# Twelve source-row tiles of each graph layer fetched row by row by SyncE

## The chip, the cores and the metric

The kernel runs on one core of one Trainium2 chip. The metric is the device time of one launch in microseconds (us). The kernel before takes 4936.72 us, the median of 3 runs (4935.95 to 4943.19).

## The reference, cut to what matters

Node features x are 12500 x 256, and there are 200000 edges (src, dst, edge_weight), sorted by dst. The graph block has two layers of this form, followed by normalizations and a residual:

```python
def _hconv(x, src, dst, ew, w1, b1, w2, b2, g, b):
    h = jax.nn.relu(x @ w1 + b1)
    msg = ew[:, None] * h[src]                                  # one row of h for each edge
    agg = jax.ops.segment_sum(msg, dst, num_segments=x.shape[0])
    h = agg @ w2 + b2
    return jax.nn.relu(_bn(h, g, b))
```

Behind it comes a mixture of 8 experts, each with three products of 256 x 256 over all nodes, weighted by a softmax. All is in 32-bit floats; the large products of the experts and with w2 are made of three partial products of split operands.

## The kernel before, in words

The stages follow one another: `first_layer` (layer norm, the product with w1, h to DRAM, and the edge tables), `aggregate(0)`, `second_layer`, `aggregate(1)`, and then `experts`, which takes the rest. The change touches the tables and the two aggregations.

Edges are cut into tiles of 128 (P), and four tiles (GT) make a group of 512 edges: 1563 tiles, 391 groups. Destinations grow quadratically, so the first groups go to few nodes. Those are treated in another way: layer 0 treats 112 groups so, layer 1 128 (FGL). For them the kernel builds dense weight sheets ("front", in DRAM), and SyncE loads them in batches: `load(a)` (L985) loads four blocks of 128 rows of h (L998) and the matching part of a sheet (L1000) into one of two buffers. TensorE's `unit` (L1067) multiplies one block; the last unit of a batch frees the buffer (semaphore f_mm), for which the load after the next waits (L995). A pass over the nodes is 25 batches; layer 0 has 4 passes, layer 1 has 5.

The other groups (279 in layer 0, 263 in layer 1, numbered q) go through gathers. GpSimd's `gather(t)` (L1020) fetches the 128 rows of h that tile t needs with one indirect DMA (L1025), into one of 16 slots (R). Before it overwrites a slot it waits for the product of the group that used it (semaphore g_mm). VectorE builds one-hot matrices with the edge weights (L1263, L1269); TensorE multiplies rows and one-hots of a group (L1109) when all four tiles have landed; VectorE adds the sums to `agg` (L1389) at an offset that it loads into registers, sixteen at a time (L1372, L1373).

The order is written at build time. `place(level)` assigns each unit to a group q, so that TensorE's estimated work per group is level; `unit_at` holds the result. TensorE's program is then, for each q: the products of the group, the products that build sheets (L1063, in the early groups), the units assigned to q, and late in the layer the products with w2. SyncE's program in an aggregation is only `for n in range(NF): load(n)`.

The edge tables src_col, rel_col and ew_col have four parts of GW = 512 columns, one column for each group; 391 of the 512 are used.

Of the kernel before, what the change touches and what calls it, by code (L numbers as in the profile page):

```python
def build(nc, a, out):
# [8 lines left out]
    P = 128  # L10
# [8 lines left out]
    GT = 4  # L19
# [3 lines left out]
    GW = GB * P  # L23
    NB = -(-N // P)
# [68 lines left out]
    def sem(name):  # L93
        return top.enter_context(nc.semaphore(name))
# [58 lines left out]
    with top:  # L153
# [65 lines left out]
        def first_layer():  # L219
            with ExitStack() as s:  # L220
# [79 lines left out]
                with nc.Block() as block:  # L300
# [88 lines left out]
                    def _(g):  # L389
# [5 lines left out]
                        for i in range(NCH + 4):  # L395
# [40 lines left out]
                            if I_TURN <= i < I_TURN + NT:  # L436
                                what, bs = turns[i - I_TURN]
                                dstbuf = {"src": src_col, "ew": ew_col, "dst": rel_col, "front": None}[what]
                                g.wait_ge(side_p, TURNS + i - I_TURN + 1)
                                for n, gb in enumerate(bs):  # L440
                                    if what == "front":
                                        ins = g.activation(
                                            (key_col, low_col)[n][:, :].rearrange("p (j f) -> p j f", f=FG),
                                            pT[(i - 1) % 2][:, n * GE:(n + 1) * GE].rearrange("p (j f) -> p j f", f=P)[:, :, 0:FG],
                                            ACT.Copy)
                                        continue
                                    ins = g.activation(
                                        dstbuf[:, :].rearrange("p (j q) -> p j q", q=GW)[:, :, gb * P:(gb + 1) * P],
                                        pT[(i - 1) % 2][:, n * GE:(n + 1) * GE].rearrange("p (j q) -> p j q", q=P), ACT.Copy)
                                ins.then_inc(turn_a, 1)  # L450
# [262 lines left out]
        ga = [sem(f"g_ga{i}") for i in range(R)]  # L713
        g_eq, g_oh, g_mm, g_add = sem("g_eq"), sem("g_oh"), sem("g_mm"), sem("g_add")
# [12 lines left out]

        def gathered_value(layer, t):

            return 16 * (layer * len(range(t % R, NTL[0], R)) + t // R + 1)  # L730

# [101 lines left out]

        ADD_SEQ = [[k for i in used for k in range(SHEET_S[i], SHEET_S[i + 1])] for used in USED]
# [54 lines left out]
        def aggregate(layer):  # L889
# [3 lines left out]
            with ExitStack() as s:  # L893
                G = ([w[:, k, :] for w in wst for k in range(KC)] + [xr[:, j, :] for j in range(TPC)]
                     + [u[:, k, i * C:(i + 1) * C] for k in range(KC) for i in range(CH // C)])
                assert len(G) == R
                OH_all = sb(s, f"oh{layer}", [P, RO, P])
# [28 lines left out]
                work_w = max(2 * AB_W + 2 * HB_W, GT * GW + 2 * GW)  # L926
# [21 lines left out]
                rel_w = work[:, 0:GT * GW]  # L948
                rel_e, ew_e = sb(s, f"{t}_rel_e", [P, 1]), sb(s, f"{t}_ew_e", [P, 1])
                base_f = work[0:1, GT * GW:GT * GW + GW]  # L950
                base_w = work[0:1, GT * GW + GW:GT * GW + 2 * GW].bitcast(i32)
# [23 lines left out]
                with nc.Block() as block:  # L975
                    @block.sync
                    def _(g):
# [25 lines left out]
                        for n in range(NF):  # L1003
                            load(n)
# [14 lines left out]
                    def _(g):  # L1019
                        def gather(t):  # L1020
                            e = F0[layer] + t
                            col = e % GT * GW + e // GT
                            if t % GT == 0 and t >= R:
                                g.wait_ge(g_mm, E0 + t // GT - RG + 1)
                            g.indirect_dma_start(G[t % R], None, h_dram[layer], bass.IndirectOffsetOnAxis(  # L1025
                                ap=src_col[:, col:col + 1], axis=0)).then_inc(ga[t % R], 16)
# [3 lines left out]
                        for t in range(NT_):  # L1030
                            gather(t)
                        g.wait_ge(g_mm, E0 + NQ)

                        def tile(q, j):
                            g.tensor_copy(far_idx[:, :], src_col[:, bass.ds(q + j * GW, 1)]).then_inc(far_sem["idx"], 1)
# [14 lines left out]
                    def _(g):  # L1050
                        def hot_products(t):
# [47 lines left out]
                        for q in range(NQ):  # L1099
# [148 lines left out]
                    def _(g):  # L1248
                        def edge_cols(x, q):

                            f, n = FGL[layer] + q, len(tiles_of[q])
                            return x[:, :].rearrange("p (j g) -> p j g", g=GW)[:, 0:n, f:f + 1].broadcast_to([P, n, width(f)])
# [100 lines left out]
                        ew_made = ew_col[:, :].rearrange("p (j g) -> p j g", g=GW)[:, :, made_g[0]:made_g[-1] + 1]  # L1353
# [70 lines left out]
                        def tile(q, j):  # L1424
                            done(g.tensor_copy(rel_e[:, :], rel_w[:, bass.ds(q + j * GW, 1)]))
                            done(g.tensor_copy(ew_e[:, :], ew_col[:, bass.ds(q + j * GW, 1)]))
# [839 lines left out]
```

## Time and profile before

| what | value |
| --- | --- |
| median of 3 runs | 4936.72 us (4935.95 to 4943.19) |
| profiled execution, its own time | 4928.61 us |
| span of its instructions | 4926.5 us |
| TensorE (PE) busy | 4481.6 us, 91% |
| VectorE (DVE) busy | 2557.4 us, 52% |
| ScalarE (ACT) busy | 2205.4 us, 45% |
| GpSimd (POOL) busy | 2257.0 us, 46% |

The shares are means over stages with different limits. Times inside the execution count from its first instruction. "Issue" is time in which an engine waited for nothing that the profile shows. A name with q (SPq, DVEq) is the engine's sequencer: DMA issues and register instructions. wst, f_xr and f_u are the buffers in which the 16 slots of gathered rows lie.

### The profile page before, as it was taken

The page shows a single profiled execution, that of the slowest core. Times are in us where ns is not written, and L with a number is a line of the kernel's source. Part 1 is how long each engine was busy: PE and PEld are TensorE (multiplying, and loading weights), DVE is VectorE, ACT ScalarE, POOL GpSimd, SP SyncE. Part 2 cuts the span into 40 slices and gives each one's busy share as a digit, 9 for nine tenths or more (in the row PEclk, how much of TensorE's full clock was granted, in tenths as well). Part 3 has the DMA queues.
Part 4 walks back from the last instruction along what each step waited for, and adds up shares of the span by engine and source line. Part 5 has one row for each costly group of instructions (what it writes and reads, how often), then busy time and mean ns, then how long its engine had stood idle before and what let it go on. Part 6 is the DMA issues. An engine that isn't in the chain of part 4 may idle for free. (4 is left out here: it accounts for less than half of the span.)

```text
span 4926.5 us, 70224 instructions
## 1 busy us (share of the span) xinstructions
PE 4481.6 (91%) x25653; PEld 3772.4 (77%) x25653; DVE 2557.4 (52%) x5644; ACT 2205.4 (45%) x3514; POOL 2257.0 (46%) x2376
## 2 busy tenths in 40 slices
PE   7779999899998589999999998499999999999999
PEld 6778888887666578778766666388888888888888
DVE  7667677773323655311222223566566656665665
ACT  5644455551100543100000000477777777777777
POOL 1477777777777367777777777500000000000000
PEclk9889999999999799999999998699999999999999
DMA  5578867797555278877666675311101110111010
GB/s 163 172 245 286 279 228 250 254 283 250 196 195 163 68 245 309 280 252 253 233 224 227 230 234 170 113 29 35 26 27 35 35 26 26 35 35 26 27 30 16
DMA packets 593000, 764.71 MB, mean 155 GB/s; under 512 B 151441, under 2 KB 484732, under 8 KB 586255
## 3 DMA queue, kind: packets, MB, share of 16 engines
q1 hardware_dynamic: 328176, 370.54, 22.5%
q0 software_dynamic: 105552, 286.55, 18.4%
q10 hardware_dynamic: 158926, 103.10, 6.9%
q8 instruction: 207, 3.39, 0.3%
q14 instruction: 139, 1.13, 0.1%
HBM read 606.69 MB, written 140.70 MB: 152 GB/s over the span
## 5 line engine op out<-in xcount | busy, mean ns | idle before, releaser
L1025 POOL DMA_INDIRECT wst<-h,src_col x1088 | 1075.0, 988 | 331.8 <-issue 325.5
L1077 PE MATMUL pf<-work 128*128 128x308 f32 (+4 forms) x3528 | 1146.2, 461 | 24.7 <-DMA work<-front 24.7
L1077 PEld LDWEIGHTS pf<-work 128*128 128x128 f32 x3528 | 648.2, 193 | 278.7 <-issue 128.1
L2069 DVE TENSOR_TENSOR f_hl<-f_hf,f_hh 128x1024 fp32r<-128x1024 f32 (+1 forms) x400 | 479.9, 1200 | 635.3 <-ACT f_hf L1932 634.8
L1925 ACT ACTIVATE f_hh<-f_p,f_sh,f_sc 128x512 fp32r<-128x512 f32 (+1 forms) x800 | 570.9, 767 | 396.7 <-PE f_p L2167 394.8
L1109 PEld LDWEIGHTS ps<-oh,wst 128*128 128x128 f32 x4352 | 556.5, 198 | 192.1 <-DMA wst<-h,src_col 121.4
L1109 PE MATMUL ps<-oh,wst 128*128 128x128 f32 x4352 | 585.9, 286 | 121.9 <-DMA wst<-h,src_col 111.0
L1223 ACT ACTIVATE ah<-agg 128x1024 fp32r<-128x1024 f32 (+1 forms) x50 | 51.8, 1037 | 1438.6 <-DVE agg L1389 1438.0
L1025 POOL DMA_INDIRECT f_xr<-h,src_col x542 | 531.7, 981 | 167.1 <-issue 161.5
L1025 POOL DMA_INDIRECT f_u<-h,src_col x536 | 529.2, 987 | 163.4 <-issue 160.3
L1389 DVE TENSOR_TENSOR agg<-agg,ps 128x60 f32 (+27 forms) x386 | 100.7, 261 | 907.7 <-PE ps L1109 880.3
L1932 ACT ACTIVATE f_hf<-f_p,f_sh,f_sc 128x512 f32<-128x512 f32 (+1 forms) x800 | 571.3, 773 | 0.0
L1307 DVE TENSOR_TENSOR agg<-agg,px 128x686 f32 (+4 forms) x512 | 352.8, 689 | 61.1 <-issue 32.9
L1389 DVE TENSOR_TENSOR agg<-agg,px 128x132 f32 (+21 forms) x156 | 45.1, 289 | 583.7 <-PE px L1109 583.5
L2081 DVE SCALAR_TENSOR_TENSOR f_x<-f_p,f_gate,f_x 128x256 f32<-128x256 f32 x784 | 324.3, 476 | 2.4 <-PE f_p L2222 2.4
L2222 PE MATMUL f_p<-Wo_hi,f_hh 128*128 128x256 f32 (+1 forms) x1568 | 317.2, 284 | 2.3 <-DVE f_x L2081 2.1
L2222 PE MATMUL f_p<-Wo_lo,f_hh 128*128 128x256 f32 (+1 forms) x1568 | 314.3, 282 | 0.0
L2222 PE MATMUL f_p<-Wo_hi,f_hl 128*128 128x256 f32 (+1 forms) x1568 | 314.0, 282 | 0.0
L2222 PEld LDWEIGHTS f_p<-Wo_hi,f_hh 128*128 128x128 f32 (+1 forms) x1568 | 250.3, 189 | 26.1 <-issue 11.2
L2167 PE MATMUL f_p<-f_hh,W_hi 128*128 128x512 f32 (+1 forms) x800 | 252.9, 397 | 1.2 <-ACT f_hf L1932 1.2
L2167 PE MATMUL f_p<-f_yh,W_hi 128*128 128x512 f32 (+1 forms) x800 | 247.8, 391 | 4.4 <-DVE f_yl L2020 2.4
L2167 PE MATMUL f_p<-f_yl,W_hi 128*128 128x512 f32 (+1 forms) x800 | 246.5, 389 | 0.0
(279 smaller groups left out, 7575.5 us busy)
## 6 DMA issues: line engine op xcount, KB each, us to landing
work<-h SPq DMA_DIRECT2D x216, 512.0 KB
work<-front SPq DMA_DIRECT2D x50, 1024.0 KB
front<-agg ACTq DMA_DIRECT2D x24, 1600.0 KB, 11.1
work<-front SPq DMA_DIRECT2D x50, 616.0 KB
work<-front SPq DMA_DIRECT2D x50, 576.0 KB
work<-front SPq DMA_DIRECT2D x50, 512.0 KB
front<-agg ACTq DMA_DIRECT2D x8, 2400.0 KB, 16.9
work<-front SPq DMA_DIRECT2D x25, 768.0 KB
```

The lines of the kernel that those rows point to most:

```text
L1025: g.indirect_dma_start(G[t % R], None, h_dram[layer], bass.IndirectOffsetOnAxis(ap=src_col[:, col:col + 1], axis=0)).then_inc(ga[t % R], 16)
L1077: ins = g.matmul(pF[:, k, 0:count * w].rearrange("p (s c) -> p s c", c=w), HB[a % 2][0:r, n, k * P:(k + 1) * P], x, start=b == 0, stop=b = ...
L1109: ins = g.matmul(pS[bank_of[q]][:, k, :], G[t % R][:, k * P:(k + 1) * P], OH[t % RO], start=t == tiles_of[q][0], stop=t == tiles_of[q][-1])
L1223: g.activation(AH[n % 2][:, :, 0:nn], agg[:, :, c * CH:c * CH + nn], ACT.Copy).then_inc(z_hi, 1)
L1307: g.tensor_tensor(v, v, x, ALU.add).then_inc(hot_a, 1)
L1389: g.tensor_tensor(win, win, pS[bank_of[q]][:, :, 0:wide], ALU.add).then_inc(g_add, 1)
L1925: ins = g.activation(hhi[l][q % 2][:, m, 0:nn], p[:, m, 0:nn], ACT.Relu, bias=shift[l][:, col], scale=scale[l][:, col])
L1932: ins = g.activation(hf[l][:, m, 0:nn], p[:, m, 0:nn], ACT.Relu, bias=shift[l][:, col], scale=scale[l][:, col])
L2069: g.tensor_tensor(hlo[l][q % 2][:, :, 0:nn], hf[l][:, :, 0:nn], hhi[l][q % 2][:, :, 0:nn].bitcast(fp32), ALU.subtract).then_inc(f_lo[l], 1)
L2081: ins = g.scalar_tensor_tensor(X1[0:r, j, :], p3[0:r, j, :], gate[c % 2][0:r, j, e:e + 1], X1[0:r, j, :], ALU.mult, ALU.add)
L2167: ins = g.matmul(o[:, m, 0:nn], ww[:, k, m * P:(m + 1) * P], xx[:, k, 0:nn], start=i == 0 and k == 0, stop=i == 2 and k == KC - 1)
L2222: ins = g.matmul(p3[0:r, j, :], x[:, k, j * P:j * P + r], w[:, k, :], start=n == 0 and k == 0, stop=n == 2 and k == KC - 1)
```

## The change

A group in a list `direct_q` (twelve for each layer) gets its last tile in another way: SyncE loads eight row numbers into registers and issues one DMA of 1 KB for each row, into one of two buffers `direct`. GpSimd leaves these tiles out, and its slots are numbered over the tiles that remain. SyncE's program becomes a list `sp_plan` of row fetches and batch loads in turn. The plan counts time in groups: 0.1 for a row, 0.3 for a load; it puts at least twelve rows before each load, and more where it sees time; a tile is used five groups after its rows are done. The row numbers come by a DMA of 512 bytes into `index_row`. Before it fills a buffer again, SyncE waits for the product that used it. TensorE waits on two semaphores for a direct tile, in place of one for a gathered one. The tables' parts shrink from 512 to 392 columns (TW).

Evaluated for these sizes, direct_q is 19, 43, 65, 86, 107, 128, 149, 169, 190, 208, 229, 250 in layer 0 and 22, 41, 60, 76, 92, 109, 125, 143, 163, 185, 206, 227 in layer 1. Layer 0 fetches 189 rows before its first load, layer 1 twelve; from then on 12 rows stand before most loads and 18 before some (in a few places more), until the last tile is done.

```diff
+    TW = NG + NG % 2
...
-        src_col = sb(edges, "src_col", [P, GT * GW], i32)
-        rel_col = sb(edges, "rel_col", [P, GT * GW])
-        ew_col = sb(edges, "ew_col", [P, GT * GW])
+        src_col = sb(edges, "src_col", [P, GT * TW], i32)
+        rel_col = sb(edges, "rel_col", [P, GT * TW])
+        ew_col = sb(edges, "ew_col", [P, GT * TW])
...
+        PARTS = 2
+        direct_in = [[sem(f"direct_in{i}_{x}") for x in range(PARTS)] for i in range(2)]
+        index_in = [sem(f"index_in{i}") for i in range(2)]
...
+        ROW_Q, LOAD_Q, ROWS_PER_LOAD, DIRECT_GAP = 0.1, 0.3, 12, 5
+        direct_q, sp_plan = [], []
+        for layer in range(2):
+            def may_load(x):
+                p, hg = divmod(x, NHG)
+                stored = 0
+                if hg == 0 and USED[layer][p] in MADE[layer]:
+                    stored = hot_q[layer][seg_end(layer, SEG_SEQ[layer].index(SHEET_S[USED[layer][p] + 1] - 1)) - 1] + 2
+                if x < 2:
+                    return stored
+                p2, hg2 = divmod(x - 2, NHG)
+                return max(stored, unit_at[layer][p2 * NB + min((hg2 + 1) * HG, NB) - 1] + 1)
+            at, plan, qs, row = 1.0, [], [], 0
+            for batch in range(NFL[layer] + 1):
+                until = may_load(batch) if batch < NFL[layer] else unit_at[layer][-1]
+                count = max(min(ROWS_PER_LOAD, NFL[layer]), int((until - at) / ROW_Q * 0.7))
+                while count > 0:
+                    if row == 0:
+                        if len(qs) >= 2:
+                            if qs[-2] + 2 > max(until, at):
+                                break
+                            at = max(at, qs[-2] + 2)
+                        if at + P * 2 * ROW_Q > unit_at[layer][-1]:
+                            break
+                    n = min(count, P - row)
+                    plan.append(("rows", len(qs), row, n))
+                    at, row, count = at + n * ROW_Q, row + n, count - n
+                    if row == P:
+                        qs.append(math.ceil(at) + DIRECT_GAP)
+                        row = 0
+                if batch < NFL[layer]:
+                    plan.append(("load", batch))
+                    at = max(at, until) + LOAD_Q
+            if row:
+                plan = [x for x in plan if x[0] == "load" or x[1] < len(qs)]
+            assert all(x < y for x, y in zip(qs, qs[1:])) and qs[-1] < NQL[layer] - 1
+            direct_q.append(qs)
+            sp_plan.append(plan)
+        pool_seq = [[t for t in range(NTL[layer]) if not (t % GT == GT - 1 and t // GT in direct_q[layer])] for layer in range(2)]
+        pool_at = [{t: n for n, t in enumerate(seq)} for seq in pool_seq]
+        def gathered_value(layer, t):
+            n = pool_at[layer][t]
+            return 16 * (layer * len(range(n % R, len(pool_seq[0]), R)) + n // R + 1)
+        def direct_value(layer, n):
+            return 16 * P // PARTS * (layer * len(range(n % 2, len(direct_q[0]), 2)) + n // 2 + 1)
...
+                direct = [sb(s, f"direct{layer}_{i}", [P, C])[:, :] for i in range(2)]
+                index_row = sb(s, f"index{layer}", [1, 2 * P], i32)
+                def rows_of(t):
+                    if t in pool_at[layer]:
+                        return G[pool_at[layer][t] % R]
+                    return direct[direct_q[layer].index(t // GT) % 2]
...
-                        for n in range(NF):
-                            load(n)
+                        row_regs = [g.alloc_register(f"{t}_row{i}") for i in range(8)]
+                        def indices(n):
+                            lo = (FGL[layer] + direct_q[layer][n]) * GE + (GT - 1) * P
+                            g.dma_start(index_row[0:1, n % 2 * P:(n % 2 + 1) * P],
+                                        a["src"][lo:lo + P].rearrange("(o e) -> o e", o=1)).then_inc(index_in[n % 2], 16)
+                        def fetch(n, first, count):
+                            if first == 0:
+                                g.wait_ge(index_in[n % 2], 16 * (layer * len(range(n % 2, len(direct_q[0]), 2)) + n // 2 + 1))
+                                if n + 1 < len(direct_q[layer]):
+                                    indices(n + 1)
+                                if n >= 2:
+                                    g.wait_ge(g_mm, E0 + direct_q[layer][n - 2] + 1)
+                            for lo in range(first, first + count, len(row_regs)):
+                                k = min(len(row_regs), first + count - lo)
+                                g.load(row_regs[0:k], index_row[0:1, n % 2 * P + lo:n % 2 * P + lo + k])
+                                for i in range(k):
+                                    row = g.snap(row_regs[i], min_val=0, max_val=N - 1)
+                                    g.dma_start(direct[n % 2][lo + i:lo + i + 1, :], h_dram[layer][bass.ds(row, 1), :]).then_inc(
+                                        direct_in[n % 2][(lo + i) * PARTS // P], 16)
+                        indices(0)
+                        for what, n, *some in sp_plan[layer]:
+                            if what == "load":
+                                load(n)
+                            else:
+                                fetch(n, *some)
...
-                            col = e % GT * GW + e // GT
-                            if t % GT == 0 and t >= R:
-                                g.wait_ge(g_mm, E0 + t // GT - RG + 1)
-                            g.indirect_dma_start(G[t % R], None, h_dram[layer], bass.IndirectOffsetOnAxis(
-                                ap=src_col[:, col:col + 1], axis=0)).then_inc(ga[t % R], 16)
+                            col = e % GT * TW + e // GT
+                            n = pool_at[layer][t]
+                            if n >= R and (n == R or pool_seq[layer][n - R] // GT != pool_seq[layer][n - R - 1] // GT):
+                                g.wait_ge(g_mm, E0 + pool_seq[layer][n - R] // GT + 1)
+                            g.indirect_dma_start(rows_of(t), None, h_dram[layer], bass.IndirectOffsetOnAxis(
+                                ap=src_col[:, col:col + 1], axis=0)).then_inc(ga[n % R], 16)
 
                         g.iota(steps, pattern=[[1, WIN_W]], base=0, channel_multiplier=0,
                                allow_small_or_imprecise_dtypes=True).then_inc(steps_set, 1)
-                        for t in range(NT_):
+                        for t in pool_seq[layer]:
...
+                        def arrived(t):
+                            if t in pool_at[layer]:
+                                g.wait_ge(ga[pool_at[layer][t] % R], gathered_value(layer, t))
+                            else:
+                                n = direct_q[layer].index(t // GT)
+                                for part in direct_in[n % 2]:
+                                    g.wait_ge(part, direct_value(layer, n))
...
-                                        g.wait_ge(ga[t % R], gathered_value(layer, t))
-                                    ins = g.matmul(pS[bank_of[q]][:, k, :], G[t % R][:, k * P:(k + 1) * P], OH[t % RO],
+                                        arrived(t)
+                                    ins = g.matmul(pS[bank_of[q]][:, k, :], rows_of(t)[:, k * P:(k + 1) * P], OH[t % RO],
```

## Rows read from the trace of the kernel before

**Rows 1.** The page, busy tenths in 40 equal slices, of TensorE and GpSimd.

```profile
PE   7779999899998589999999998499999999999999
...
POOL 1477777777777367777777777500000000000000
```

**Rows 2.** Stretches: busy us (x) of PE, PEld, DVE, ACT, POOL; clock, DMA share, GB/s.

```profile
167.00:1622.00 1455.00, 1304.23 (x7546) 1096.18 (x7547) 820.20 (x1953) 552.41 (x1099) 1112.85 (x1116) 0.95 0.72 233
1763.00:3106.00 1343.00, 1222.15 (x6686) 971.49 (x6686) 387.34 (x1050) 139.43 (x200) 1022.85 (x1052) 0.96 0.72 241
400.00:450.00 50.00, 49.66 (x322) 44.63 (x321) 36.35 (x78) 27.26 (x53) 38.27 (x39) 1.00 0.87 280
2225.00:2390.00 165.00, 152.18 (x917) 136.57 (x916) 31.00 (x102) 3.94 (x4) 125.19 (x131) 0.98 0.78 258
```

**Rows 3.** GpSimd's timeline: start, length, instruction, idle before it.

```profile
2300.33 0.95 POOL L1025 DMA_INDIRECT wst<-h,src_col  x1 [0.30 <-issue]
```

**Rows 4.** Costliest lines: busy, mean ns, idle before, what ended it.

```profile
L1025 POOL DMA_INDIRECT wst<-h,src_col x1088 | 1075.0, 988 | 331.8 <-issue 325.5 <-PE px L1109 4.3 <-PE ps L1109 2.1
```

**Rows 5.** The same view, TensorE's products of gathered rows.

```profile
L1109 PE MATMUL ps<-oh,wst 128*128 128x128 f32 x4352 | 585.9, 286 | 121.9 <-DMA wst<-h,src_col 111.0 <-DVE oh L1269 10.0
L1109 PE MATMUL px<-oh,f_xr 128*128 128x128 f32 x1256 | 176.5, 292 | 38.1 <-DMA f_xr<-h,src_col 37.6
```

**Rows 6.** Waits of SyncE's queue: us in total, times, longest.

```profile
SPq L998 <- PE pf L1077: 2166.2, 217, 30.2
...
SPq L993 <- DMA front<-agg: 162.7, 1, 162.7
```

**Rows 7.** Register instructions: ns min/median/max, first and last start.

```profile
L1373 DVEq MOVE  x542: 36/36/36, 175.1 to 3105.9; - x181
L1389 DVEq FUSED_REGOPS  x542: 46/46/53, 186.2 to 3109.7; - x181
L1372 DVEq TENSOR_LOAD <-base_row x35: 1041/1100/4019, 173.8 to 3074.9; - x35
L959 SPq TENSOR_LOAD <-far x2: 486/488/490, 1538.6 to 2999.9; - x2
```

**Rows 8.** SyncE's timeline at two places: start, length, DMA issue.

```profile
1762.66 0.23 SPq L982 DMA_DIRECT2D w_raw<-front_windows  x1
1762.93 0.39 SPq L998 DMA_DIRECT2D work<-h  x1
...
1783.92 0.36 SPq L998 DMA_DIRECT2D work<-h  x1
...
2226.22 0.56 SPq L1000 DMA_DIRECT2D work<-front  x1
...
2235.63 0.51 SPq L1000 DMA_DIRECT2D work<-front  x1
...
2241.18 0.32 SPq L1000 DMA_DIRECT2D work<-front  x1
```

**Rows 9.** The 32 KB block copies in the expert stage.

```profile
L1835 SPq DMA_DIRECT2D wst<-wst x384: 585/611/1975, 3195.9 to 4839.3; - x192
```

**Rows 10.** Batch loads, four passes; last line: waited for in 2226:2382.

```profile
L1000 SPq DMA_DIRECT2D work<-front x23: 365/614/1578, 947.9 to 1156.2; - x23
L1000 SPq DMA_DIRECT2D work<-front x23: 506/524/1584, 1784.3 to 1991.2; - x23
L1000 SPq DMA_DIRECT2D work<-front x23: 367/507/1472, 2020.6 to 2189.0; - x23
L1000 SPq DMA_DIRECT2D work<-front x23: 320/506/556, 2226.2 to 2380.5; - x23
  PE pf L1077: 3.9, 6
```

**Rows 11.** DMA view of 2226:2381: queue; issues with landing time.

```profile
q1 hardware_dynamic: 14785, 23.07, 44.1%
...
wst<-h,src_col POOLq DMA_INDIRECT x62, 4.2
```

More of the change, by code:

```diff
@@ L447, in _ @@
                                     ins = g.activation(
-                                        dstbuf[:, :].rearrange("p (j q) -> p j q", q=GW)[:, :, gb * P:(gb + 1) * P],
-                                        pT[(i - 1) % 2][:, n * GE:(n + 1) * GE].rearrange("p (j q) -> p j q", q=P), ACT.Copy)
+                                        dstbuf[:, :].rearrange("p (j q) -> p j q", q=TW)[:, :, gb * P:min((gb + 1) * P, TW)],
+                                        pT[(i - 1) % 2][:, n * GE:(n + 1) * GE].rearrange("p (j q) -> p j q", q=P)[
+                                            :, :, 0:min(P, TW - gb * P)], ACT.Copy)
                                 ins.then_inc(turn_a, 1)
@@ L726, in build @@
         z_out = sem("z_out")
-        def gathered_value(layer, t):
-            return 16 * (layer * len(range(t % R, NTL[0], R)) + t // R + 1)
         NFL = [NHG * len(used) for used in USED]
@@ L925, in aggregate @@
                 w2h, w2l = (sb(s, f"w2{layer}_{n}", [P, KC, C], f32r)[:, :, :] for n in ("hi", "lo"))
-                work_w = max(2 * AB_W + 2 * HB_W, GT * GW + 2 * GW)
+                work_w = max(2 * AB_W + 2 * HB_W, GT * TW + 2 * GW)
                 work = sb(s, f"work{layer}", [P, work_w])
@@ L947, in aggregate @@
                 far_idx = sb(s, f"{t}_idx", [P, 1], i32)
-                rel_w = work[:, 0:GT * GW]
+                rel_w = work[:, 0:GT * TW]
                 rel_e, ew_e = sb(s, f"{t}_rel_e", [P, 1]), sb(s, f"{t}_ew_e", [P, 1])
-                base_f = work[0:1, GT * GW:GT * GW + GW]
-                base_w = work[0:1, GT * GW + GW:GT * GW + 2 * GW].bitcast(i32)
+                base_f = work[0:1, GT * TW:GT * TW + GW]
+                base_w = work[0:1, GT * TW + GW:GT * TW + 2 * GW].bitcast(i32)
                 def take(g, name):
@@ L1034, in tile @@
                         def tile(q, j):
-                            g.tensor_copy(far_idx[:, :], src_col[:, bass.ds(q + j * GW, 1)]).then_inc(far_sem["idx"], 1)
+                            g.tensor_copy(far_idx[:, :], src_col[:, bass.ds(q + j * TW, 1)]).then_inc(far_sem["idx"], 1)
                             take(g, "idx")
@@ L1251, in edge_cols @@
                             f, n = FGL[layer] + q, len(tiles_of[q])
-                            return x[:, :].rearrange("p (j g) -> p j g", g=GW)[:, 0:n, f:f + 1].broadcast_to([P, n, width(f)])
+                            return x[:, :].rearrange("p (j g) -> p j g", g=TW)[:, 0:n, f:f + 1].broadcast_to([P, n, width(f)])
                         def onehot_rows(q):
@@ L1424, in tile @@
                         def tile(q, j):
-                            done(g.tensor_copy(rel_e[:, :], rel_w[:, bass.ds(q + j * GW, 1)]))
-                            done(g.tensor_copy(ew_e[:, :], ew_col[:, bass.ds(q + j * GW, 1)]))
+                            done(g.tensor_copy(rel_e[:, :], rel_w[:, bass.ds(q + j * TW, 1)]))
+                            done(g.tensor_copy(ew_e[:, :], ew_col[:, bass.ds(q + j * TW, 1)]))
                             g.tensor_scalar(OH[0], lane[:, :], rel_e[:, :], ew_e[:, :], ALU.is_equal,
```

2 lines of the change are left out of this document (1 added, 1 removed).

## The prediction

> **What bounds the kernel now.** I read the page first (shares by engine, the 40 slices), then the busy time by stretch, then who waited for whom on GpSimd and TensorE, then SyncE's own queue. The page [rows 1] shows TensorE busy nearly everywhere and GpSimd busy only in two blocks, slices 4 to 13 and 15 to 26: these are the two aggregations, the only stretches that the change touches. The chain that ended last lies in the expert stage behind them and says nothing of them, so I read the aggregations by stretches and by waits.
>
> In the aggregations GpSimd issues one iota and then gathers alone: 1115 in 1455 us and 1051 in 1343 us, which is 1.305 and 1.278 us for each [rows 2]. One gather holds it about 0.95 us and 0.30 us of issue follow [rows 3]. In the largest of the three groups of gathers (1088 of 2166) the idle time is 331.8 us, of which 325.5 are that issue, part of its own pace, and only 4.3 + 2.1 are waits for TensorE [rows 4]; the two others are alike. So GpSimd runs almost without a stop from the first gather to the last. TensorE is busy 1304 of 1455 and 1222 of 1343 us [rows 2], and what it waits for there is gathered rows: 111.0 and 37.6 us in the two largest of its five groups of products [rows 5]. The reading: GpSimd's gather stream sets the pace, and TensorE has about a tenth to spare, unevenly spread. SyncE's queue is idle: it waits 2166 us for TensorE to free a batch buffer [rows 6].
>
> **The change, part by part.**
>
> *24 gathers leave GpSimd.* Evaluated with N = 12500 and E = 200000, the new plan gives twelve groups in each layer (19, 43, 65, ... 250 and 22, 41, 60, ... 227) whose last tile is no longer gathered. GpSimd is spared 12 × 1.305 + 12 × 1.278 = 31.0 us, and as it has no stop to hide them, all of it lies on the path. Everything after shifts forward with the end of each layer. The slot numbering by n % 16 keeps sixteen slots, with at most one tile more of lead, counted at nothing.
>
> *3072 rows are added to SyncE.* A row is a register move, the register arithmetic of the address, and a DMA of 1 KB. In the trace a move takes 36 ns and fused register operations 46 ns [rows 7], on VectorE; SyncE's smallest DMA (one descriptor) takes 0.23 us, and the next one starts 0.04 us after it ends (1762.66 + 0.23 to 1762.93) [rows 8]. I take 0.036 + 0.046 + 0.23 + 3 × 0.04 = 0.43, rounded to 0.44 us a row. No DMA with an address from a register is in the trace. Lower end: the register operations cost nothing, 0.27 us. Upper end: the DMA costs as much as the 32 KB block copies, 0.61 us [rows 9], with more register operations around it, 0.82 us. I stay close to the low end, since the one-descriptor DMA is the nearest row. Before each eight rows there is a register load: one register takes 0.49 us on SyncE, a batch of up to sixteen 1.10 us on VectorE (4.0 at worst) [rows 7]; I take 0.7 us for eight and 0.6 for four, with bounds 0.5 and 1.3.
>
> Twelve rows, the minimum that the plan puts before each load, thus take 12 × 0.44 + 1.3 + 2 × 0.04 = 6.7 us. A load's two DMAs take 0.37 + 0.04 + 0.51 + 0.04 = 0.96 us [rows 8]. So SyncE needs 7.6 us a load: 5.2 at the lower ends (12 × 0.27 + 1.0 + 0.96), 13.4 at the upper (12 × 0.82 + 2.6 + 0.96).
>
> The Trainium skill, Runtime: NRT & Kernel Launch, section Instruction fetch mechanics, puts a register load at some 200 ns for each register, even in bulk. By that eight and four would take 1.6 and 0.8 us and the load cycle 8.7 us. The row disagrees: at most 1.10 / 16 = 0.07 us a register in the usual case, although it is VectorE's row and the rule speaks of loads from HBM.
>
> *What stands behind the rows on SyncE.* Only the batch loads, and TensorE's blocks wait for them. Today a load is issued the moment its buffer is free; afterwards it is late whenever SyncE's cycle is longer than the distance between two loads. The mean distances follow from the first and last start of 23 loads each [rows 10]: layer 0, third pass 9.5 us; layer 1, first pass 9.4 us, second 7.65 us ((2189.0 - 2020.6) / 22), third 7.01 us ((2380.5 - 2226.2) / 22). In the other passes the loads are over 10 us apart, and where the plan has up to 18 rows a load, over 12: 18 × 0.44 + 1.9 + 0.12 + 0.96 = 10.9 us fit. At 7.6 us every pass fits but the third of layer 1, with the second just at the edge: 22 × (7.6 - 7.01) = 13 us of lateness builds up there.
>
> *What absorbs lateness.* In those passes a batch is used as soon as it has landed (TensorE waits for it 6 times, 3.9 us in all [rows 10]), so a late load is a late TensorE. But GpSimd is not stopped until its sixteen slots are full: 16 × 1.28 = 20.5 us, less one group's four gathers (5.1), the landing (4.2 [rows 11]) and the group's products (some 2 us), leaves about 9 us. TensorE wins the lag back later with its spare tenth. So 13 us cost about 4; uneven distances (9.4 and then 5.6 us, starts 2226.22, 2235.63, 2241.18 [rows 8]) I put at 2 more, an estimate. Loss 6 us, 0 at the lower end; at the upper end all of (13.4 - distance) × 22 over the four closest passes, less their cushions: 88 + 126 + 140 + 86 - 36 = 404 us.
>
> *Start of a layer.* In layer 1 the first load is issued at 1762.93 today; after the change an index DMA, its landing, a register load and 12 rows come first, about 10 us, and the second load comes 7 us later still. The first batch is freed at 1783.9 [rows 8]. TensorE is some 5 us late there, within the 9 us: nothing. In layer 0 189 rows (some 100 us) precede the first load, but that one waits 162.7 us for the first stores anyway [rows 6]: nothing.
>
> *Waits that are added.* SyncE waits for the product of the direct tile before last; the plan puts the rows behind it, and it is over when the next load is allowed. TensorE waits for a direct tile, planned five groups (5 × 5.1 = 26 us) ahead of its use: nothing, up to some us each if SyncE is late. Its two waits in place of one are 24 × 0.05 us. The tables of 392 columns shorten three copies in the first stage, off the gather stream: nothing either way.
>
> Sum: -31.0 + 6 = -25 us. The profiled execution took 4928.61 us (span 4926.5), so it would take 4904; it is 8.1 us under the median of 4936.72, on which I put the same difference: 4912 us.
>
> **Rivals.**
>
> *A: a row costs more, and SyncE becomes the bound of layer 1 (slower).* With 0.15 us more a row, which is one or two register operations and a slower DMA, the cycle is 7.6 + 1.8 = 9.4 us. Second pass: 22 × 1.75 - 9 = 29.5; third pass: 22 × 2.39 - 9 = 43.6 us. Loss 73, net +42: 4979 us. It cancels the gain where 22 (c - 7.65) + 22 (c - 7.01) - 18 = 31, at c = 8.4 us, that is at 0.51 us a row. For it: no row shows a DMA with a register address, and the block copies take 0.61. Against: the smallest DMAs take 0.23. By the skill's price for register loads alone the cycle would be 8.7, and the result about 4949.
>
> *B: TensorE takes over.* In a hot stretch it is busy 49.66 of 50 us [rows 2]. If it set the pace for half of the time, half of the gain remains: 15.5 - 6, 4927 us. Against: GpSimd hardly waits there today.
>
> *C: one DMA engine gets all the rows.* A row is one piece of 1 KB; if it is not split, it is one of the 16 engines' work. In the third pass SyncE's queue has 14785 packets for 44.1% of 16 engines over 155 us, 74 ns each [rows 11]: twelve add 0.9 us every 7 us on an engine that is busy 0.78 of the time [rows 2], so batches and gathers end 1 us later, and if that engine fills up, pass after pass. Price 0 to 40 us, 4945 in the middle. The Trainium skill, DMA: Bandwidth & Descriptors, section Why a DMA increments its semaphore by 16 and not by 1, says that such a DMA goes to the lowest-numbered engine and not around all of them; the packed rows here don't tell engines apart.
>
> **Chances.** Forecast 0.52, A 0.28, B 0.13, C 0.07. Two executions can be told apart from about 0.2%, 10 us. Faster: 0.52 + 0.08 of B = 0.60; same: 0.03 of A, 0.05 of B, 0.03 of C = 0.11; slower: 0.25 of A, 0.04 of C = 0.29. The range goes from the full gain with a little more (4904) to rival A with its price nearly doubled (4985); the forecast's own range is 4904 to 4925.
>
> **What would show it.** GpSimd: 2142 gathers, still about 1.28 us each, both aggregations shorter by 12 to 15 us. SyncE: row period 0.44 us, register loads 0.6 to 0.7; load starts in the third pass of layer 1 7.0 to 7.6 us apart. TensorE: waits for work<-front up by less than 30 us, for the direct tiles near 0. If a row takes over 0.51 us, the second and third passes of layer 1 grow and the forecast is wrong by rival A; if rows are at 0.44 and the gathers don't end earlier, by B.

## The result, and the profile after

The changed kernel takes 5090.8 us (median of 6 runs, 5082.0 to 5096.2) against 4936.6 us: 1.0307 times as long, 95% interval 1.0294 to 1.0320, 154 us slower. The forecast was 4912 us, the upper end of the range 4985. The profiled execution took 5096.2 us with a span of 5094.4.

The page of the changed kernel, busy tenths in 40 slices (answers to [rows 1]):

```profile
PE   7778889888998589887799999579999999999999
...
POOL 1577667766777467665577777620000000000000
```

GpSimd no longer holds its 7 throughout. Three stretches of the changed kernel, columns as in [rows 2]: the two aggregations and the third pass of layer 1.

```profile
167.00:1684.00 1517.00, 1316.08 (x7538) 1100.74 (x7539) 818.64 (x1953) 551.70 (x1099) 1099.76 (x1104) 0.93 0.69 223
1820.00:3272.00 1452.00, 1254.77 (x6688) 993.64 (x6688) 388.81 (x1050) 140.55 (x201) 1017.84 (x1040) 0.94 0.67 224
2333.00:2557.00 224.00, 171.54 (x935) 151.54 (x934) 31.99 (x107) 3.94 (x4) 129.61 (x136) 0.89 0.59 194
```

The reader is to see that the aggregations grew by 62 and 109 us, and that in the third pass TensorE was busy 171.5 of 224 us (77%; before 152.2 of 165, 92%) and the DMA engines 0.59 (0.78): all are less busy, so something else is late. The mean granted clock of that stretch, where 1 is 2.4 GHz, fell from 0.98 to 0.89, and TensorE idled more there. For nearly the same number of products TensorE was also busy longer, 1316.1 after 1304.2 us in layer 0 and 1254.8 after 1222.2 in layer 1, 44 us together, at a mean granted clock of 0.93 after 0.95 and of 0.94 after 0.96. That comes on top of the waits, and how much of it lengthened the path was not measured apart; my sum had no term for it.

Two of the costliest lines of the changed kernel, TensorE's blocks of the batches and GpSimd's largest group of gathers:

```profile
L1177 PE MATMUL pf<-work 128*128 128x308 f32 (+4 forms) x3528 | 1194.5, 475 | 209.5 <-DMA work<-front 209.4
L1116 POOL DMA_INDIRECT wst<-h,src_col x1072 | 1062.5, 991 | 431.4 <-issue 316.6 <-PE px L1209 61.0 <-PE ps L1209 53.8
```

TensorE waits 209.4 us for batches; it was 24.7 us. GpSimd, which had waited 4.3 + 2.1 us in this group [rows 4], now waits 61.0 + 53.8. The gathers themselves are unchanged (0.991 us each, 0.988 before). SyncE's queue, which had waited 2166 us for TensorE to free a buffer [rows 6], waits for it 283.7 us now:

```profile
SPq L1061 <- PE pf L1177: 283.7, 65, 17.8
...
SPq L1056 <- DMA front<-agg: 36.8, 1, 36.8
```

And what fills it, each instruction of a row and the register load (answers to [rows 7, 8]), columns as in [rows 7]:

```profile
L1085 SPq FUSED_REGOPS  x3072: 44/44/59, 169.3 to 3062.8; - x192
...
L1086 SPq MOVE direct<-h x3072: 29/29/37, 169.4 to 3062.8; - x192
L1086 SPq DMA_DIRECT2D direct<-h x3072: 224/228/1260, 169.4 to 3062.9; - x192
...
L1083 SPq TENSOR_LOAD <-index x510: 462/1168/8722, 168.4 to 3061.5; - x170
```

A row's three instructions are 44, 29 and 228 ns; in the trace one row starts 0.42 us after the other in the median, where I had put 0.44. The register load has a median of 1.17 us and a maximum of 8.72; the 510 take 753 us together. I had put 0.7 for eight and 0.6 for four, some 330 us in all.

The batch loads of the same four passes as in [rows 10] (layer 0 third; layer 1 first, here without one load, second, third), and in the last line who waited in the last of them:

```profile
L1063 SPq DMA_DIRECT2D work<-front x23: 376/498/1631, 980.5 to 1226.5; - x23
L1063 SPq DMA_DIRECT2D work<-front x22: 497/500/1703, 1856.4 to 2066.7; - x22
L1063 SPq DMA_DIRECT2D work<-front x23: 377/498/1382, 2104.6 to 2313.3; - x23
L1063 SPq DMA_DIRECT2D work<-front x23: 378/497/512, 2350.2 to 2556.5; - x23
...
  PE pf L1177: 56.1, 19
```

In the third pass a load comes every (2556.5 - 2350.2) / 22 = 9.38 us, after 7.01; in the second every 9.49 us, after 7.65. TensorE waits 19 times there, 56.1 us, after 6 times and 3.9. And SyncE itself does not wait once in the third pass: its own work sets the pace.

**Two lengths of one instruction.** The register loads of the changed kernel in three passes: layer 1 first, layer 1 third, layer 0 fourth.

```profile
L1083 SPq TENSOR_LOAD <-index x48: 487/710/2742, 1831.8 to 2062.1; - x48
L1083 SPq TENSOR_LOAD <-index x52: 547/1209/1880, 2323.2 to 2556.9; - x52
L1083 SPq TENSOR_LOAD <-index x56: 540/1856/1975, 1236.5 to 1520.2; - x56
```

Sorted by the number of registers, loads of eight take 0.72 us (0.79 before the first batch) or 1.86 to 1.95, loads of four 0.58 or 1.13, and little between. The first pass of layer 1 has the short ones. There the plan's blocks begin at rows 0, 12, 24 and so on, all multiples of four. Later a block of 22 rows moves the start to row 90, and from then on most starts are 1, 2 or 3 words off a multiple of four (a tile's first load, at row 0, never is); in layer 0 the block of 61 rows does it. In all 371 of the 510 loads start off a multiple of four. One, two or three words off, loads of eight take the same 1.86 to 1.87 us in the median. Loads of one, two and three registers take some 0.6, 0.73 and 0.92 us wherever they start, so that a load of four from a multiple of four, 0.58, is cheaper than one of two. That gave theory M: a register load whose first word is not at a multiple of 16 bytes is read register by register. Theory W: it waits for the batch DMA issued just before it. Theory E: the one-row DMAs crowd one DMA engine (rival C).

### The profile page after: what moved, and what is told of

It is laid out like the page before. It is cut to its first block and busy times, and to the rows that moved or that the text cites. A ratio compares the mean times of both kernels' runs of the same rounds, so it can differ in the third digit from the quotient of the medians.

```text
span 5094.4 us, 79978 instructions
## 1 busy us (share of the span) xinstructions
PE 4530.2 (89%) x25653; PEld 3803.2 (75%) x25653; DVE 2556.9 (50%) x5644; ACT 2205.0 (43%) x3514; POOL 2238.0 (44%) x2352
## 3 DMA queue, kind: packets, MB, share of 16 engines
q1 hardware_dynamic: 334368, 373.71, 21.9%
## 5 line engine op out<-in xcount | busy, mean ns | idle before, releaser
L1177 PE MATMUL pf<-work 128*128 128x308 f32 (+4 forms) x3528 | 1194.5, 475 | 209.5 <-DMA work<-front 209.4
L1116 POOL DMA_INDIRECT wst<-h,src_col x1072 | 1062.5, 991 | 431.4 <-issue 316.6
L1177 PEld LDWEIGHTS pf<-work 128*128 128x128 f32 x3528 | 665.6, 199 | 487.1 <-DMA work<-front 236.6
L1209 PE MATMUL ps<-oh,wst 128*128 128x128 f32 x2640 | 374.6, 283 | 39.8 <-DVE oh L1369 21.1
L1209 PEld LDWEIGHTS ps<-oh,wst 128*128 128x128 f32 x2640 | 350.3, 199 | 68.9 <-DMA wst<-h,src_col 24.0
L1209 PE MATMUL ps<-oh,f_xr 128*128 128x128 f32 x1872 | 299.6, 293 | 56.7 <-DMA f_xr<-h,src_col 54.2
L1209 PEld LDWEIGHTS ps<-oh,f_xr 128*128 128x128 f32 x1872 | 267.0, 205 | 91.9 <-DMA f_xr<-h,src_col 60.6
L2322 PEld LDWEIGHTS f_p<-Wo_hi,f_hh 128*128 128x128 f32 (+1 forms) x1568 | 251.0, 189 | 25.9 <-issue 11.2
L1209 PEld LDWEIGHTS px<-oh,wst 128*128 128x128 f32 x1648 | 217.3, 199 | 62.4 <-DMA wst<-h,src_col 38.3
```

Of the source, the lines that this page charges most:

```text
L1116: g.indirect_dma_start(rows_of(t), None, h_dram[layer], bass.IndirectOffsetOnAxis(ap=src_col[:, col:col + 1], axis=0)).then_inc(ga[n % R], 16)
L1177: ins = g.matmul(pF[:, k, 0:count * w].rearrange("p (s c) -> p s c", c=w), HB[a % 2][0:r, n, k * P:(k + 1) * P], x, start=b == 0, stop=b = ...
L1209: ins = g.matmul(pS[bank_of[q]][:, k, :], rows_of(t)[:, k * P:(k + 1) * P], OH[t % RO], start=t == tiles_of[q][0], stop=t == tiles_of[q][-1])
L2322: ins = g.matmul(p3[0:r, j, :], x[:, k, j * P:j * P + r], w[:, k, :], start=n == 0 and k == 0, stop=n == 2 and k == KC - 1)
```

## The experiments

Medians with the median of the kernel before, run beside them on the same chip, and the ratio with its 95% interval.

**Rounded counts** (label aligned), all starts at multiples of four, still 24 tiles:

```diff
                 count = max(min(ROWS_PER_LOAD, NFL[layer]), int((until - at) / ROW_Q * 0.7))
+                count -= count % 4
```

> The number of rows before each batch load is rounded down to a multiple of four, so every register load starts at a row number whose place in index_row is a multiple of four (16 bytes). Still twelve tiles a layer. Theory M (a register load that does not start at a multiple of 16 bytes is read register by register): in the trace of the changed kernel loads of eight take 0.72 to 0.79 us where they start at a multiple of four and 1.86 to 1.95 where they don't, loads of four 0.58 and 1.13. Then all are at 0.7 and 0.6 here, outside the front stores, the load cycle is 12 x 0.42 + 0.72 + 0.58 + 0.06 + 0.96 = 7.3 us, the third pass of layer 1 is back near 7.0 to 7.5 us a load, and the time is 4905 to 4925 us. Rival W (a register load waits for the batch DMA that was just issued): the first load after each batch load stays at 1.86 us, and the time stays within 20 us of 5091. Rival E (the one-row DMAs crowd one DMA engine): registers get faster, but TensorE goes on waiting for work<-front and the time stays over 5000 us.

Measured: 4948.7 us against 4937.4, ratio 1.0023 (1.0014 to 1.0032). 142 us of the loss are gone. Loads of eight take 0.72 us in the median and loads of four 0.58, right behind a batch load too; only some beside the front stores are longer. W falls. But the time is above the 4905 to 4925 that M had; 40 us are unexplained by the register loads, taken up below.

**The same plan, index_row 8 bytes later** (shifted):

```diff
-                index_row = sb(s, f"index{layer}", [1, 2 * P], i32)
+                index_row = sb(s, f"index{layer}", [1, 2 * P + 4], i32)[:, 2:2 + 2 * P]
```

> The kernel with rounded counts, but index_row begins two elements later, so that every register load starts 8 bytes behind a multiple of 16. The plan, the rows and the waits are those of the kernel with rounded counts. Theory M: all loads of eight take 1.9 us and all of four 1.13 us, a load cycle of 9.0 us in the dense passes, and the time is over 5090 us, perhaps 5110, since now the first passes are slow too. Rival W: register loads as in the kernel with rounded counts, and the same time within 10 us.

Measured: 5107.3 us against 4937.4, ratio 1.0349 (1.0332 to 1.0366). One edit, of 8 bytes, costs 159 us. The register loads of the two kernels, rounded counts first and shifted second:

```profile
L1084 SPq TENSOR_LOAD <-index x467: 465/713/3051, 168.2 to 2947.4; - x156
```

```profile
L1084 SPq TENSOR_LOAD <-index x467: 1030/1859/7801, 166.5 to 3097.3; - x156
```

The same 467 loads, 0.71 against 1.86 us in the median, 375 against 868 us in all. Who waits for the batches follows, TensorE's row of the waits (sum in us, waits, longest), the rounded kernel first and the shifted one second:

```profile
PE pf L1178 <- DMA work<-front: 81.4, 38, 7.0
```

```profile
PE pf L1178 <- DMA work<-front: 206.7, 75, 12.6
```

Theory M's condition is shown: it is the place of the first word that counts, and nothing else was changed. A load of eight takes 0.09 us a register on a boundary of 16 bytes and 0.23 off it. That the registers are then read one by one fits the steps from one to three registers above, but no run shows it.

**The gain by itself** (gain_only): the 24 gathers are left out and nothing is fetched.

```diff
-                    return direct[direct_q[layer].index(t // GT) % 2]
+                    return G[pool_at[layer][t - 1] % R]
...
-                                fetch(n, *some)
```

> GpSimd leaves out the same 24 gathers, but nothing fetches those tiles: TensorE multiplies the rows of the tile before instead, without a wait, and SyncE issues batch loads alone. That part of the sums is not the reference's. It measures the gain term by itself. If the gather stream sets the pace: 31 us less than before, 4906 us (4903 to 4912). If TensorE would take over soon (rival B): 4915 to 4925. If GpSimd does not bound at all: 4936.

Measured: 4904.4 us against 4937.4, ratio 0.9933 (0.9918 to 0.9948): 33 us, where the sum had 31.0. The gather stream does set the pace, and GpSimd still hardly waits for TensorE (6.1 + 1.5 us in the group below). Rival B falls. The largest group of gathers of this kernel, columns as in [rows 4]:

```profile
L1114 POOL DMA_INDIRECT wst<-h,src_col x1072 | 1064.2, 993 | 327.3 <-issue 319.7 <-PE ps L1206 6.1 <-PE px L1206 1.5
```

**Rows at fixed addresses** (static_rows): all 3072 row DMAs, no registers. A DMA reads row 97 × (its place in the tile), so that every tile reads the same 128 rows of h.

```diff
-                                g.load(row_regs[0:k], index_row[0:1, n % 2 * P + lo:n % 2 * P + lo + k])
...
-                                    row = g.snap(row_regs[i], min_val=0, max_val=N - 1)
+                                    row = 97 * (lo + i)
```

> The changed kernel's plan with its 3072 one-row DMAs, but each reads a row of h that is fixed when the kernel is built: no register loads, moves or address arithmetic. The rows are not the reference's. A row then costs 0.22 + 0.04 = 0.27 us, twelve 3.2 us, the load cycle 4.2 us. Theory M or W (the register loads are the cost): no lateness, 4905 to 4912 us. Rival E (one DMA engine is crowded by the rows, however they are issued): TensorE waits for work<-front by 50 us or more over before, and the time is over 4950 us.

Measured: 4906.7 us against 4937.4, ratio 0.9934 (0.9919 to 0.9949). Within 2.3 us of the kernel without any row, and TensorE waits for batches 32.9 us (24.7 before). The row DMAs of this kernel, with nothing between them on SyncE:

```profile
L1085 SPq DMA_DIRECT2D direct<-h x3072: 214/252/1485, 167.2 to 2871.8; - x192
```

So the row transfers cost nothing that can be told apart, rival C falls, and the loss is in the time that SyncE spends on registers: the loads, and 0.12 us a row (0.42 against 0.295 from row to row) for the move and the arithmetic.

**Eight rows a load** (rows8), which leaves 10 and 9 tiles:

```diff
-        ROW_Q, LOAD_Q, ROWS_PER_LOAD, DIRECT_GAP = 0.1, 0.3, 12, 5
+        ROW_Q, LOAD_Q, ROWS_PER_LOAD, DIRECT_GAP = 0.1, 0.3, 8, 5
...
-                count = max(min(ROWS_PER_LOAD, NFL[layer]), int((until - at) / ROW_Q * 0.7))
+                count = max(ROWS_PER_LOAD if batch >= 2 else 0, int((until - at) / ROW_Q * 0.7))
+                count -= count % 4
```

> As the kernel with rounded counts, but eight rows at least and none forced before the first two loads of a layer: 10 and 9 tiles. Load cycle 5.1 us in the dense passes. Lateness theory: no batch load is late by over 1 us in the mean, 19 x 1.29 = 24.5 us less than before, 4911 to 4917. If something else than late loads costs the rounded kernel its gain: 4930 or more.

Measured: 4912.5 us against 4934.9, ratio 0.9950 (0.9937 to 0.9964): 22 us faster than the kernel before, with 24.5 expected. Its batch loads in the third pass of layer 1, and TensorE's waits for batches in the whole:

```profile
L1064 SPq DMA_DIRECT2D work<-front x23: 361/498/732, 2211.2 to 2364.0; - x23
```

```profile
PE pf L1178 <- DMA work<-front: 35.6, 18, 6.5
```

A load comes every (2364.0 - 2211.2) / 22 = 6.95 us again (7.01 before, 9.38 in the changed kernel).

**More rows where the plan sees time** (rows8_more): LOAD_Q 0.2, 0.9 in place of 0.7, counts in eights; 30 tiles.

> Eight rows (not twelve) at least before each load, counts in eights so that each register load takes eight from a multiple of 16 bytes, none forced before the first two loads of a layer, a load planned at 0.2 groups and 0.9 of the free time used. 16 and 14 tiles. The load cycle is 8 x 0.42 + 0.72 + 0.06 + 0.96 = 5.1 us in the dense passes, where it fits (5.2 us is the shortest distance before). If the lateness of loads is all that took the gain: 30 x 1.29 = 39 us less, minus some 3 to 8: 4900 to 4910. If more rows in the sparse passes (up to 24 a load, 12 us) are late themselves or their tiles are awaited: 4915 to 4930.

Measured: 5007.8 us against 4934.9, ratio 1.0138 (1.0122 to 1.0153). A miss by 100 us, on a kernel whose register loads all start on a boundary: TensorE waits 146.2 us for batches, and in the first pass of layer 0 SyncE issues its loads 7 us late in the mean. The expectation had taken eight rows a load for the close passes. The plan put more there: 14.2 before a load in the third pass of layer 0 and in the first of layer 1, 12.0 and 10.5 in the second and third of layer 1, and 20.0 in the first pass of layer 0. With them these passes are 19, 22, 8, 14 and 28 us longer than in gain_only. In the first pass of layer 0 SyncE's own work takes 13.9 us a load, where the loads were 12.6 us apart, and it waits for a buffer once. By the medians of its instructions that would be 11.8 us; the rest is the longer instructions beside the front stores (last section), so there it takes both. In the second and third pass of layer 1 hardly any instruction is longer, and the further rows are left as the cause. No run takes the two apart.

**No rows before the first two loads** (late_start), and **index_row on partition 64** (partition64), both on the rounded kernel:

```diff
-                count = max(min(ROWS_PER_LOAD, NFL[layer]), int((until - at) / ROW_Q * 0.7))
+                count = max(ROWS_PER_LOAD if batch >= 2 else 0, int((until - at) / ROW_Q * 0.7))
```

```diff
-                index_row = sb(s, f"index{layer}", [1, 2 * P], i32)
+                index_row = sb(s, f"index{layer}", [P, 2 * P], i32)[64:65, :]
```

> The kernel with rounded counts and twelve rows, but no rows forced before the first two loads of a layer. In its trace the first pass of layer 1 ends some 10 us later than where nothing is fetched. If that comes from the 12 + 12 rows before the first two loads: 8 to 12 us less than the rounded kernel, 4937 to 4941. If the first pass is slow because its register loads are hit by the front stores: within 3 us of the rounded kernel.

> The kernel with rounded counts, but index_row lies on partition 64 and not on 0. In the traces register loads within 9 us of a front store are longer (up to 8.7 us), also VectorE's. If the store's reads or SyncE's batch writes crowd partition 0 alone, loads of eight stay at 0.72 us here throughout, and the time falls by 5 us against the rounded kernel. If it is contention of all of SBUF or of the sequencers' path to it: the same lengths, the same time.

Measured: 4946.3 and 4948.5 us against 4934.9, ratios 1.0025 (1.0015 to 1.0034) and 1.0023 (1.0013 to 1.0032). Against the rounded kernel's ratio, 1.0023, both are nothing. The 8 to 12 us that the first theory of late_start had did not come: the rows before the first loads cost little, as the prediction had it. And the long register loads are not a matter of partition 0.

**Eight rows a load, all register loads slow** (rows8_shifted; the edit of index_row as in shifted, on rows8):

> The kernel with eight rows a load, index_row again two elements later, so that every register load is of the slow kind (1.87 us for eight). The load cycle is 8 x 0.42 + 1.87 + 0.06 + 0.96 = 6.2 us, below the closest mean distance of 6.9 us. If register loads cost only through the cycle of SyncE: a few us of lateness at the short distances (5.2 us) and at the front stores, which the lead of GpSimd absorbs, so within 12 us of the aligned kernel of eight rows (4912): 4913 to 4924. If slow register loads cost in another way too (their reads disturb other engines' accesses, or each adds its length to the path, 313 x 1.15 = 360 us over both layers): over 4935.

Measured: 4922.1 us against 4931.8, ratio 0.9982 (0.9973 to 0.9991). The register loads are 1.87 us again, 0.72 in rows8, and they cost some 13 us by the medians (22.4 us under the kernel before in rows8, 9.7 here), 16 by the ratios, and not 360: TensorE's waits for batches in rows8_shifted:

```profile
PE pf L1178 <- DMA work<-front: 57.2, 28, 12.4
```

They rise from 35.6 to 57.2 us only. The length of a register load counts where it makes SyncE's cycle longer than a distance between loads.

**Twelve rows only where loads are over 10 us apart** (mixed), the other edits as in rows8:

> Eight rows a load in the third pass of layer 0 and in the first three of layer 1, twelve elsewhere, where loads are over 10 us apart: 11 and 10 tiles. Two tiles more than the kernel of eight rows: by the cycle of 7.3 us against 10 us nothing is late, so 2.6 us less than it, 4910 (4905 to 4914). If the front stores' long register loads in the first passes of layer 0 make twelve rows late there: 4912 to 4920.

Measured: 4908.7 us against 4931.8, ratio 0.9952 (0.9939 to 0.9966). The same as rows8 within the intervals; the two further tiles, 2.6 us, are below what these runs can tell.

**The tables alone** (tables_only), 392 columns and nothing else of the change:

> The kernel before with edge tables of 392 columns and nothing else changed. All theories: within 3 us of the kernel before; three copies in the first stage are shorter and all else is the same. A difference over 5 us would mean that the place of other tiles in SBUF counts, and would have to be taken off the other results.

Measured: 4932.8 us against 4931.8, ratio 0.9999 (0.9990 to 1.0009). Nothing, as forecast.

## Why the prediction was wrong, step by step

*GpSimd's 31 us:* right. Shown by gain_only, 33 us.

*A row at 0.44 us:* right, 0.42. The nearest row was the right one to take, and a register address does not lengthen the DMA (0.228 us in the median; 0.23 was taken).

*Register loads at 0.7 and 0.6 us:* this is the term that failed. On a boundary of 16 bytes they take 0.72 and 0.58, as taken; the plan puts 371 of the 510 off it, where eight registers take 1.86 and four 1.13. VectorE's sixteen in 1.10 us [rows 7], my row for the price, all start at multiples of sixteen columns of base_row: a row that shows only one case of an instruction. The upper bound of 1.3 us was made from that row too and did not hold. Twelve rows then take 12 × 0.42 + 1.86 + 1.13 + 0.1 = 8.1 us, and with the load's 0.96 the cycle is 9.1 us, where I had 7.6; measured 9.38 in the third pass. This is rival A's mechanism, by another term than the one I gave it (a dearer row), and its point of decision, 8.4 us, was passed. The Trainium skill, Runtime: NRT & Kernel Launch, section Instruction fetch mechanics, has some 200 ns a register, for loads from HBM; the loads from SBUF off the boundary agree (0.23), those on it do not (0.09). I had set that rule aside by VectorE's row.

*The lateness of the loads:* its size was wrong with the cycle, and where SyncE is only just fast enough, the way of reckoning was wrong too. The table sets SyncE's cycle, as each kernel's own trace has it, against the distances of the trace of before, over the third to the last load of a pass. "Mean" is 22 × (cycle - mean distance), my way. "Each" is the sum of max(0, cycle - distance) over the 22 loads, each with its own cycle and distance.

| kernel, pass | mean distance | cycle | loads that waited | mean | each | measured |
| --- | --- | --- | --- | --- | --- | --- |
| changed, layer 0, first | 12.62 | 14.4 | 0 | 39 | 52 | 38.5 |
| changed, layer 0, third | 9.47 | 11.2 | 0 | 38 | 49 | 41.8 |
| changed, layer 1, first | 9.40 | 9.1 | 10 | 0 | 19 | 9.6 |
| changed, layer 1, second | 7.65 | 9.5 | 1 | 40 | 46 | 42.6 |
| changed, layer 1, third | 7.01 | 9.4 | 0 | 52 | 55 | 55.3 |
| rounded, layer 0, first | 12.62 | 10.3 | 19 | 0 | 2 | 0 |
| rounded, layer 0, third | 9.47 | 9.1 | 8 | 0 | 18 | 8.2 |
| rounded, layer 1, first | 9.40 | 9.1 | 10 | 0 | 21 | 9.7 |
| rounded, layer 1, second | 7.65 | 7.8 | 4 | 3 | 21 | 7.2 |
| rounded, layer 1, third | 7.01 | 7.8 | 2 | 16 | 27 | 23.4 |

(us. Cycle is the time from load to load less SyncE's waits for a freed buffer; of 22 loads, so many had such a wait. Measured is the time from the third to the last load of the pass, less that of gain_only, one trace each.)

In the changed kernel SyncE waits once, for 0.3 us, in four of the five passes. It is the bound there, and so the mean with the cycle that the trace shows must give nearly all: 168 of the 188 us that the five passes lost, and those are nearly all of the 195 us between the spans of this kernel and of gain_only. So what failed for the 154 us is the cycle. In the rounded kernel it is the reckoning as well. By the lengths of its instructions its cycle is 12 × 0.42 + 0.72 + 0.58 + 0.06 + 0.96 = 7.4 us, less than my 7.6, and yet it loses 44 us to gain_only (4948.7 - 4904.4), where my sum had 6. Two things make that up. Its cycle is really 7.8 us in the second and third pass of layer 1, and 9.1 in the two passes in which front stores run. And SyncE waits at a long distance and is late at a short one, and the one does not pay for the other: the mean gives 19 of the 48 us of these passes. The sum over each load gives 88, too much, as it does in rows8_shifted, whose third pass of layer 1 has 12 us by it (cycle 6.6 us) and lost 0.2. So the truth lies between. It seems that part of a single late load is taken up again, by the lead that I had granted or by TensorE's spare time; that is argued, and I did not test which.

*Layer 0, first and third pass, 38.5 and 41.8 us:* I had called the first safe, with 18 rows in 10.9 us. With slow register loads 18 rows are 7.6 + 2 × 1.86 + 0.73 + 0.1 + 0.96 = 13.1 us against 12.62, but the pass had 15 rows a load in the mean, and its cycle was 14.4:

```profile
L1063 SPq DMA_DIRECT2D work<-front x23: 376/503/1532, 348.2 to 664.5; - x23
```

Very long instructions make the rest (last section): its 56 register loads took 125 us, where by the medians of their kinds they would take 80, and its 330 row DMAs 19 us more than at 0.228 each. Without these 64 us the cycle would be 11.5 us, under the distance. In the third pass it is 20 + 18 us, and without them the cycle would be 9.5, just the distance. In the rounded kernel the first pass had such an excess too, 15 + 19 us, and lost nothing. So in layer 0 it took both, the starts off the boundary and the long instructions.

*Direct tiles late, slots, tables, start of layer 1:* right, near nothing. TensorE has no wait for a direct tile in the changed kernel's trace; tables_only and late_start show the others.

*Rivals:* A happened, at 5091 and not 4979 us, as its price left out layer 0 and the register loads; B and C are refuted.

*A reading of the page:* GpSimd's first block of work begins in slice 2, with 4 tenths, and not in slice 4 [rows 1]. Nothing in the sum rests on it.

## What to carry to other kernels

When work is given to an idle queue, compare its new cycle with the distances between the jobs that stand behind it, stretch by stretch: a queue that waits 2166 us in total had its jobs only 7.0 us apart in one pass. Where the cycle is longer than the mean distance, the difference times the jobs is the loss, to within a tenth or so here. Where it is only near the distance, the mean says too little (19 of 48 us) and the sum of max(0, cycle - distance) over the jobs too much (88); take them as the two ends, and leave room. Price an instruction by rows that cover its cases: alignment made one register load cost 0.72 or 1.86 us here, and rounding a count to four was worth 142 us. With eight rows a load and aligned starts the idea pays: 4912 us, 0.5% under the kernel before.

## What the runs showed of the hardware

- A register load (TENSOR_LOAD) of eight words from SBUF takes 0.72 us on SyncE when it starts at a multiple of 16 bytes and 1.86 when it starts 8 bytes behind (aligned and shifted), or 4 or 12 (the changed kernel); of four words 0.58 and 1.13. One, two and three words take some 0.6, 0.73 and 0.92 us in the changed kernel wherever they start.
- Register loads that start within 9 us of the issue of one of ScalarE's front stores (1.6 to 2.4 MB from SBUF) are often much longer than the others. In the kernel before, 17 of VectorE's 24 such loads took over 2.2 us (up to 4.0), and none of the 55 others; in the changed kernel 28 of SyncE's 52, against 6 of its 460 others. The row of VectorE's loads of base_row while those stores run, in the kernel before:

```profile
L1372 DVEq TENSOR_LOAD <-base_row x10: 1098/3086/4019, 352.2 to 1094.3; - x10
```

  Moving the row numbers to partition 64 changed nothing. The row DMAs of such passes are longer as well: 264 of them took 18 us more than at 0.228 us each in the third pass of layer 0, and 3 us more in the third pass of layer 1, where no front store runs. That the stores are the cause is argued from the times, not shown by a run.
- 3072 DMAs of 1 KB at fixed addresses, one 0.295 us after the other in the trace of static_rows (median), cost 2.3 us beside the batch loads against no rows at all (4906.7 - 4904.4), within the spread of the runs. A row is not split: the queue of static_rows has 6192 packets more than that of gain_only (334368 - 328176), two for each of its 3072 row DMAs and 24 DMAs of row numbers.
